# Cross-attention's steps begin behind eight units: the other batches' rows and the null terms move into steps 1 to 7

## The chip, the core and the metric

The kernel runs on one core of a Trainium2 chip. The metric is the time of one execution on the device in microseconds (us), the median of several runs. An engine works through its own queue of instructions in order and waits for semaphores: TensorE (PE in the profile, PEld its weight loads), VectorE (DVE), ScalarE (ACT) and GpSimd (POOL); SyncE (SP) issues most DMAs. PEclk, the granted clock, is the share of TensorE's full clock: 1.00 is 2.4 GHz, 0.50 is 1.2 GHz.

## The reference

One decoder block on `x` (4 batches of 256 rows, width 128) with a context of 512 rows of width 256 for each batch: layer norm, cross-attention with 16 heads of 64 and one learned null key and null value for all heads, a layer norm of its result, a residual sum; then rotary self-attention and a mixture of 8 experts. The change touches cross-attention alone:

```python
kv = jnp.einsum('bmc,cf->bmf', context, Wkv)
k, v = jnp.split(kv, 2, axis=-1)                 # 16 heads of 64
k = jnp.concatenate((nk, k), axis=-2)            # the null key in front
v = jnp.concatenate((nv, v), axis=-2)
sim = jnp.einsum('bhid,bhjd->bhij', q * scale, k)
attn = jax.nn.softmax(sim, axis=-1)
out = jnp.einsum('bhij,bhjd->bhid', attn, v)     # then @ Wout, normalised
```

All products are made in float32 accuracy: each operand is split into a rounded part (`_hi`) and a rest (`_lo`), and three products are added up.

## The kernel before

**The loop.** Cross-attention runs in steps `s` = 0 to 34, one for each pair of heads of a batch (8 pairs, 4 batches), and three to drain. The code writes each engine's queue out by hand; in a step every engine handles pieces of several pairs: scores of pairs s+1 and s+2, transposed probabilities and weighted values of pair s, the query product of pair s+2 (`project_q(s + 2)`), and one *key unit* and one *value unit* of later use (`keys_unit`, `values_unit`: six products of 128x512 each, into one PSUM bank, then a ScalarE copy `_hi` and a rest `_lo`). Its order on TensorE in the second half of a step is: value unit, weighted values of the pair before, whatever a batch needs (`finish_batch`, `null_probs`), transposes, query product, weighted values of this pair (`weighted_values(s, 0)`), scores of pair s+2. Steps that use the out bank for a third purpose put the weighted values ahead of the value unit (`values_late`), and `weighted_values(s, 0)` waits there until that third user is read (`third_user_read`). On VectorE the second half is: o_halves, q_tail(s+2), inverse_sum, `finish_batch`, probs_tail.

**The head.** The *head*, ahead of step 0, is what `class Prologue` holds: loads, the split of the weights into `wkv_hi`/`wkv_lo` in five pieces, layer norm and transposes of the rows, and a list `FIRST` of units that alternate between two banks; a unit waits until VectorE has read the unit two places earlier. `FIRST` holds four key units, four value units and two units "x" that turn the rows of tiles 2 to 7 (batches 1 to 3; batch 0's tiles 0 and 1 go first, `first_tokens`). The head also makes the *null queries* `w0` (null key times Wq), the *null scores* (rows times w0, per tile, kept as `s0n`) and the *null outputs* `u` (null value times Wout), each by products of TensorE. At its end step 0 begins with `keys_unit(0)`.

**Memory.** The raw weights and the head's scratch tiles lie where the loop's `pT_hi`, `o_raw` and others lie later, which is why ScalarE's first o_copy waits for the null outputs and for `wout_lo`.

## Time and profile before

| | us |
|---|---|
| median of 3 runs (lowest, highest) | 642.07 (641.66, 642.63) |
| the profiled execution | 644.23 |
| its span, first to last instruction | 642.4 |
| TensorE busy in the span | 564.4 (88%) |
| VectorE busy | 492.9 (77%) |
| ScalarE busy | 420.5 (65%) |
| GpSimd busy | 327.2 (51%) |

The span is one execution seen by the profiler, with 1.8 us around it. The shares are means over stages with different limits: cross-attention takes about the first 365 us, self-attention and the experts the rest. A row of a timeline gives start, length, engine, line, operation and tiles; the bracket at its end is how long the engine had been idle and who released it.

### The profile page before, as it was taken

The numbers are of one execution on the slowest core, as the hardware profiler recorded it, in microseconds if no ns is written. First come the engines' busy times: TensorE is split into PE (matmuls) and PEld (weight loads), VectorE is DVE, ScalarE is ACT, GpSimd is POOL, SyncE is SP. The second block draws the span as 40 slices with busy tenths as digits, with TensorE's granted clock in tenths as the row PEclk, the third lists the DMA queues.
The fourth block names the chain that finished last, engine by engine and source line by source line (L and its number), as shares of the span: only waits on it lengthen the run. The fifth ranks groups of instructions, "written<-read, shape, count | busy, mean of one in ns | idle before, by whom it ended". The sixth has DMA issues, their size and how long they took to land. (4 is left out here: it accounts for less than half of the span.)

```text
span 642.4 us, 11040 instructions
## 1 busy us (share of the span) xinstructions
PE 564.4 (88%) x3364; PEld 437.0 (68%) x3364; DVE 492.9 (77%) x1037; ACT 420.5 (65%) x1030; POOL 327.2 (51%) x609
## 2 busy tenths in 40 slices
PE   4799889999999898998988558999886699999996
PEld 3467668777777676776866456666555678888885
DVE  4848877887878686978689437898883589999994
ACT  4448767867678766777677427888873355666652
POOL 0517966776677865777766656376963100000000
PEclk9789999999999998999999957999998599999998
DMA  8200010000100000000000020002220000000001
GB/s 297 60 1 2 2 33 2 1 2 2 34 0 2 2 1 0 2 2 2 2 1 2 1 94 1 2 2 87 86 87 2 0 1 1 1 2 1 1 0 34
DMA packets 12186, 13.64 MB, mean 21 GB/s; under 512 B 2144, under 2 KB 10336, under 8 KB 12128
## 3 DMA queue, kind: packets, MB, share of 16 engines
q1 hardware_dynamic: 11664, 12.87, 6.3%
q8 instruction: 28, 0.46, 0.3%
q14 instruction: 30, 0.25, 0.1%
q10 hardware_dynamic: 464, 0.07, 0.1%
HBM read 12.41 MB, written 0.52 MB: 20 GB/s over the span
## 5 line engine op out<-in xcount | busy, mean ns | idle before, releaser
L1166 POOL TENSOR_SCALAR attn_probs<-attn_probs,rinv 128x512 f32<-128x512 f32 x128 | 90.8, 722 | 20.4 <-DVE rinv L1023 20.3
L858 ACT ACTIVATE attn_probs<-bank,bias 128x512 f32<-128x512 f32 x128 | 87.3, 687 | 15.3 <-DVE bias L1016 15.3
L1032 DVE TENSOR_TENSOR pT_lo<-bank,pT_hi 128x512 fp32r<-128x512 f32 x128 | 86.7, 680 | 6.6 <-ACT pT_hi L876 5.0
L688 PE MATMUL bank<-ident,attn_probs 128*128 128x128 f32 x512 | 77.9, 281 | 14.3 <-POOL attn_probs L1166 11.3
L1008 DVE TENSOR_REDUCE neg_max<-bank 128x1 f32<-128x512 f32 x128 | 83.9, 677 | 3.2 <-PE bank L671 3.2
L688 PEld LDWEIGHTS bank<-ident,attn_probs 128*128 128x128 f32 x512 | 55.5, 141 | 41.7 <-POOL attn_probs L1166 25.4
L876 ACT ACTIVATE pT_hi<-bank 128x512 fp32r<-128x512 f32 x128 | 74.2, 595 | 8.8 <-PE bank L688 7.9
L720 PE MATMUL bank<-pT_hi,vals 128*128 128x256 f32 x256 | 65.7, 289 | 2.8 <-DVE pT_lo L1032 2.0
L2008 ACT ACTIVATE act_hi<-act_f 128x512 fp32r<-128x512 f32 x56 | 35.4, 633 | 43.3 <-DVE act_f L2049 43.3
L720 PE MATMUL bank<-pT_lo,vals 128*128 128x256 f32 x256 | 63.6, 282 | 0.0
L720 PEld LDWEIGHTS bank<-pT_hi,vals 128*128 128x128 f32 x256 | 48.4, 189 | 5.4 <-DVE pT_lo L1032 2.6
L1609 ACT ACTIVATE p_raw<-s_pair,neg_max 128x128 f32<-128x128 f32 (+1 forms) x128 | 43.2, 429 | 9.7 <-DVE neg_max L1669 9.5
L720 PEld LDWEIGHTS bank<-pT_lo,vals 128*128 128x128 f32 x256 | 48.4, 189 | 0.8
L1159 POOL TENSOR_TENSOR total<-row_sum,e 128x2 f32<-128x2 f32 x64 | 15.1, 236 | 63.3 <-ACT e L865 60.3
L1042 DVE TENSOR_TENSOR o_sum<-o_raw 64x256 f32<-64x256 f32 x64 | 30.5, 477 | 15.1 <-ACT o_raw L888 13.4
L2053 DVE TENSOR_TENSOR act_lo<-act_f,act_hi 128x512 fp32r<-128x512 f32 x56 | 38.5, 687 | 1.6 <-ACT act_hi L2008 1.0
L2042 DVE TENSOR_TENSOR up_w<-u_bank,wide 128x512 f32<-128x512 f32 x48 | 33.2, 691 | 7.3 <-PE u_bank L1962 1.9
L2049 DVE TENSOR_TENSOR act_f<-up_w,gate 128x512 f32<-128x512 f32 x56 | 38.4, 686 | 0.1
L1186 POOL TENSOR_TENSOR vals<-v_raw,vals 128x512 fp32r<-128x512 f32 x28 | 36.6, 1306 | 2.3
L1669 DVE TENSOR_REDUCE neg_max<-s_pair 128x2 f32<-128x256 f32 x64 | 32.5, 551 | 3.6 <-PE s_pair L1522 3.1
L671 PE MATMUL bank<-keys_hi,q_hi 64*128 64x512 f32 x128 | 32.3, 501 | 3.0 <-ACT attn_probs L858 1.9
L2002 ACT ACTIVATE gate<-g_bank 128x512 f32<-128x512 f32 x56 | 32.6, 582 | 2.4 <-PE u_bank L1962 2.4
(303 smaller groups left out, 1586.8 us busy)
## 6 DMA issues: line engine op xcount, KB each, us to landing
ctx_raw<-in_ctx_T SPq DMA_DIRECT2D x4, 512.0 KB, 3.8
gu_raw<-in_L_ffn_w_gate SPq DMA_DIRECT2D x4, 448.0 KB, 3.5
gu_raw<-in_L_ffn_w_up SPq DMA_DIRECT2D x4, 448.0 KB, 4.4
dn_raw<-in_L_ffn_w_down SPq DMA_DIRECT2D x4, 448.0 KB, 5.3
wkv_raw<-in_L_xattn_Wkv SPq DMA_DIRECT2D x3, 512.0 KB, 9.0
wkv_raw<-in_L_xattn_Wkv SPq DMA_DIRECT2D x2, 256.0 KB, 6.8
wq_raw<-in_L_xattn_Wq SPq DMA_DIRECT2D x1, 512.0 KB, 7.1
wqT_raw<-in_wq_T SPq DMA_DIRECT2D x1, 512.0 KB, 8.2
```

What stands on the lines that cost most here:

```text
L688: last = pe.transpose(t_bank[half][:, j * N + t * P:j * N + (t + 1) * P], probs[:, g % 2, i, t, kt * P:(kt + 1) * P], k.ident[:, :])
L720: last = pe.matmul(o_part, k.vals[:, kt, 2 * (g % HP) + i, :], x[:, i, kt, :], start=kt == 0 and n == 0, stop=kt == KT - 1 and n == 1)
L858: act.activation(probs[:, g % 2, i, t, :], score_bank(G, i)[:, :], ACT.Exp, bias=bias[:, t, h:h + 1], scale=X_SCALE, accum_out=row_sum[:, ...
L876: act.activation(pT_hi[:, i, 2 * half:2 * half + 2, :], t_bank[half][:, :].rearrange("p (j n) -> p j n", j=2), ACT.Copy).then_inc(t_hi_s, 1)
L1008: dve.tensor_reduce(neg_max[:, t, h:h + 1], score_bank(G, i)[:, :], AX_X, ALU.max, negate=True).then_inc(max_s, 1)
L1032: dve.tensor_tensor(pT_lo[:, i, 2 * half:2 * half + 2, :], t_bank[half][:, :].rearrange("p (j n) -> p j n", j=2), f(pT_hi[:, i, 2 * half:2 ...
L1166: pool.tensor_scalar(probs[:, g % 2, i, t, :], probs[:, g % 2, i, t, :], rinv[:, t, h:h + 1], 1.0, ALU.mult, ALU.mult).then_inc(p_norm_s, 1)
L1186: pool.tensor_tensor(values_of(k, i, t, 1), raw, f(values_of(k, i, t, 0)), ALU.subtract).then_inc(v_lo_s, 1)
L1609: last = act.activation(p_raw[:, G % 4, j, t, 0:n], s_bank[(G % 2) * REP + j][:, t * N:t * N + n], ACT.Exp, bias=neg_max[:, t, h:h + 1])
L2008: act.activation(act_hi[:, n % 2, :], act_f[:, n % 2, :], ACT.Copy).then_inc(a_hi_s, 1)
L2049: dve.tensor_tensor(act_f[:, n % 2, :], up_w[:, n % 2, :], gate[:, n % 2, :], ALU.mult).then_inc(mul_s, 1)
L2053: dve.tensor_tensor(act_lo[:, n % 2, :], act_f[:, n % 2, :], f(act_hi[:, n % 2, :]), ALU.subtract).then_inc(a_lo_s, 1)
```

## The change

Five things change; line numbers move with them.

1. `FIRST` is four key units and four value units. The rows of batch 1, 2 and 3 are turned in steps 2, 3 and 4 (`TOKEN_STEPS`): two transposes on TensorE, two copies on ScalarE, a rest on VectorE. The null scores of tiles 2 to 7 are made in step 5, the null outputs in step 7. All use the out bank as a third user, so those steps are `values_late`, and `weighted_values(s, 0)` waits for the VectorE instruction that read it last.
2. The statistics of tiles 2 to 7 end the head on VectorE; GpSimd's inverse deviation for them moves into step 0, the normalisation of the six tiles into VectorE's step 1.
3. In the head, TensorE makes the null queries and the scores of pair 0 before the second key unit; VectorE makes all of `wq_lo` (GpSimd had three quarters); the diagonals of the null key and value are set before `cT_lo`.
4. GpSimd's `output_weights`, `residual_bias` and `self_weights` move from steps 0, 2, 3 to steps 1, 4, 5.
5. The host lays the five pieces of Wkv out so that each partition's part is contiguous, and the null key and value as one array of two columns, loaded by one DMA in place of four. Some scratch tiles move to other memory, and two waits of ScalarE in step 0 go.

```diff
-FIRST = [("k", 0, 0), ("k", 1, 0), ("x", 2, 6), ("k", 2, 0), ("v", 0, 0), ("k", 3, 0),
-         ("v", 0, 1), ("v", 0, 2), ("v", 0, 3), ("x", 6, 8)]
+FIRST = [("k", i, 0) for i in range(KT)] + [("v", 0, t) for t in range(KT)]
...
-        for i in range(2):
-            for which, col in ((0, self.nk_col), (1, self.nv_col)):
-                act.dma_start(col[i * DH:(i + 1) * DH, :], dram["L0_xattn_null_kv"][which, :].rearrange("(d o) -> d o", o=1))\
-                    .then_inc(self.null_in, 16)
+        act.dma_start(self.null_cols[:, :], dram["null_cols"]).then_inc(self.null_in, 16)
...
+        TOKEN_STEPS = {2: 1, 3: 2, 4: 3}
+        NULL_SCORES, NULL_OUTPUTS = 5, 7
+        FIRST_STEPS = (*TOKEN_STEPS, NULL_SCORES, NULL_OUTPUTS)
...
             def third_user_read(s):
 
+                if s in TOKEN_STEPS:
+                    pe.wait_ge(first.xT_lo, TOKEN_STEPS[s] + 1)
+                if s == NULL_SCORES:
+                    pe.wait_ge(first.s0_s, 2)
+                if s == NULL_OUTPUTS:
+                    pe.wait_ge(first.u_lo_s, 1)
...
+            def first_extra(s):
+
+                if s not in FIRST_STEPS:
+                    return
+                pe.wait_ge(o_raw_s, 2 * s)
+                if s in TOKEN_STEPS:
+                    first.turn_tokens(pe, TOKEN_STEPS[s])
+                if s == NULL_SCORES:
+                    first.null_scores(pe, range(QT, TT))
+                if s == NULL_OUTPUTS:
+                    first.null_outputs(pe)
...
-            first.first_tokens(pe)
+            first.turn_tokens(pe, 0)
             first.unit(pe, 0)
             project_q(0)
-            first.unit(pe, 1)
             first.null_queries(pe)
             pe.wait_ge(k.first_lo, 1)
             scores(0, 0)
-            first.null_scores(pe, range(QT), (first.x0_hi, 1)).then_inc(first.null_ps, 1)
+            scores(0, 1)
+            first.null_scores(pe, range(QT))
             project_q(1)
-            scores(0, 1)
-            for n in (2, 3, 4):
+            for n in (1, 2, 3):
                 first.unit(pe, n)
             scores(1, 0)
-            for n in range(5, len(FIRST)):
+            for n in range(KT, len(FIRST)):
                 first.unit(pe, n)
-            pe.wait_ge(first.s0_s, 1)
-            first.null_scores(pe, range(QT, TT), (k.first_hi, len(FIRST)))
-            first.null_outputs(pe)
...
             def finish_batch(s):
+                if s == 1:
+                    first.normal(dve, range(QT, TT), 2)
+                if s in TOKEN_STEPS:
+                    first.tail_tokens(dve, TOKEN_STEPS[s])
+                if s == NULL_SCORES:
+                    first.null_shift(dve, slice(QT, TT), (first.null_ps, 3))
+                if s == NULL_OUTPUTS:
+                    dve.wait_ge(first.u_hi_s, 1)
+                    dve.tensor_tensor(k.u_lo[:, :], first.pU, f(k.u_hi[:, :]), ALU.subtract).then_inc(first.u_lo_s, 1)
...
                 if s == 0:
+                    first.inverse_deviation(pool, slice(QT, TT), 2)
+                if s == 1:
                     output_weights()
-                if s == 2:
+                if s == 4:
                     residual_bias()
-                if s == 3:
+                if s == 5:
                     self_weights()
```

What it moves on the engines is seen at two places. The first is TensorE at the end of the head, from the last value unit (`wkv_hi`, `cT_hi` products) to the first key unit of step 0 (`cT_hi,wkv_hi`). Before:

```order
L86 MATMUL bank<-wkv_hi,cT_hi 128x512
L86 MATMUL bank<-wkv_hi,cT_lo 128x512
L86 MATMUL bank<-wkv_lo,cT_hi 128x512
L230 MATMUL bank<-ident,xn 128x128 x2
L259 MATMUL bank<-w,xnT 128x16 x6
L266 MATMUL bank<-wout_raw,nv_diag 16x128 x8
L84 MATMUL bank<-cT_hi,wkv_hi 128x512
```

And of the change:

```order
L86 MATMUL bank<-wkv_hi,cT_hi 128x512
L86 MATMUL bank<-wkv_hi,cT_lo 128x512
L86 MATMUL bank<-wkv_lo,cT_hi 128x512
L84 MATMUL bank<-cT_hi,wkv_hi 128x512
L84 MATMUL bank<-cT_lo,wkv_hi 128x512
L84 MATMUL bank<-cT_hi,wkv_lo 128x512
```

The last transposes, six matmuls of null scores (each two passes) and eight of null outputs are gone from between them. The second place is VectorE in the second half of steps 1 and 2, from `q_lo` of the query product to `pT_lo` of the probabilities. Before, it reads the same in both steps:

```order
L1042 TENSOR_TENSOR o_sum<-o_raw 64x256 x2
L986 TENSOR_TENSOR q_lo<-bank,q_hi 128x256
L1023 RECIPROCAL rinv<-total 128x2
L1032 TENSOR_TENSOR pT_lo<-bank,pT_hi 128x512
L1008 TENSOR_REDUCE neg_max<-bank 128x1
```

Of the change, step 1 and then step 2:

```order
L994 TENSOR_TENSOR q_lo<-bank,q_hi 128x256
L1031 RECIPROCAL rinv<-total 128x2
L275 TENSOR_SCALAR xn<-x,mean_var,rstd 128x128 x6
L1040 TENSOR_TENSOR pT_lo<-bank,pT_hi 128x512
...
L994 TENSOR_TENSOR q_lo<-bank,q_hi 128x256
L1031 RECIPROCAL rinv<-total 128x2
L235 TENSOR_TENSOR xnT_lo<-bank,xnT_hi 128x256
L1040 TENSOR_TENSOR pT_lo<-bank,pT_hi 128x512
```

The normalisation of six tiles, and in step 2 the rest of the turned rows, stand between the reciprocal and `pT_lo`, behind `q_lo`.

## Rows read from the trace of the kernel before

**Rows 1.** Windows, one per step (steps 1 to 4 and 8); columns in the first line.

```profile
core 0: us, PE busy (x) PEld busy (x) DVE busy (x) ACT busy (x) POOL busy (x), PEclk, DMA share, GB/s
50.50:59.45 8.95, 8.95 (x62) 7.16 (x61) 7.44 (x17) 7.20 (x21) 5.28 (x13) 1.00 0.01 2
59.45:69.12 9.67, 8.81 (x60) 6.99 (x59) 8.71 (x17) 7.28 (x22) 9.21 (x16) 1.00 0.00 1
69.12:79.05 9.93, 9.32 (x63) 7.29 (x61) 8.25 (x17) 7.90 (x22) 9.28 (x19) 1.00 0.01 2
79.05:90.84 11.79, 9.50 (x59) 7.20 (x60) 8.71 (x19) 7.82 (x23) 7.52 (x15) 1.00 0.15 44
...
119.10:128.54 9.44, 9.41 (x63) 7.22 (x62) 7.29 (x17) 7.30 (x22) 6.78 (x16) 1.00 0.00 0
```

**Rows 2.** Timeline of the two transfers' and the context split's start.

```profile
1.17 0.53 ACTq L179 DMA_DIRECT2D nk_col<-in_L_xattn_null_kv  x1
...
6.50 1.23 DVE L1075 TENSOR_TENSOR cT_lo<-ctx_raw,cT_hi 128x1024 fp32r<-128x1024 f32 x1 [0.82 <-ACT cT_hi L918]
```

**Rows 3.** DMA issues: operation, count, KB each, median us from issue to landing.

```profile
nk_col<-in_L_xattn_null_kv ACTq DMA_DIRECT2D x2, 0.2 KB, 5.4
```

**Rows 4.** Timeline of the head and of step 0's first keys.

```profile
12.60 0.39 PE L84 MATMUL bank<-cT_hi,wkv_hi 128*128 128x512 f32 x1
...
13.97 1.85 PE L251 MATMUL bank<-nk_diag,wqT_raw 128*128 128x16 f32 x16
...
17.91 1.84 POOL L1244 TENSOR_TENSOR wq_lo<-wq_raw,wq_hi 128x768 fp32r<-128x768 f32 x1
...
18.23 1.54 DVE L1016 SCALAR_TENSOR_TENSOR bias<-neg_max,s0n 128x2 f32<-128x2 f32 x1
...
44.34 0.69 DVE L993 TENSOR_TENSOR keys_lo<-bank,keys_hi 128x512 fp32r<-128x512 f32 x1 [2.46 <-ACT keys_hi L829]
```

**Rows 5.** VectorE's groups by line and shape, from 0 to 45 us.

```profile
L1008 DVE TENSOR_REDUCE neg_max<-bank 128x1 f32<-128x512 f32 x7 | 4.5, 680 | 0.0
L192 DVE TENSOR_TENSOR wkv_lo<-wkv_raw,wkv_hi 128x1024 fp32r<-128x1024 f32 x3 | 4.1, 1373 | 0.2 <-ACT wkv_hi L186 0.2
L219 DVE TENSOR_TENSOR vals<-bank,vals 128x512 fp32r<-128x512 f32 x4 | 2.7, 686 | 1.4 <-ACT vals L206 1.4
L284 DVE TENSOR_SCALAR xn<-x,mean_var,rstd 128x128 f32<-128x128 f32 x8 | 2.2, 336 | 1.1 <-POOL rstd L298 1.1
L64 DVE BATCH_NORM_STATS2 stats<-x 128x6 f32<-128x128 f32 x8 | 1.7, 282 | 3.2 <-DMA x<-in_x_tiles 3.2
```

**Rows 6.** Timeline of step 8's second half.

```profile
124.86 0.38 PE L756 MATMUL bank<-ident,p 128*16 128x128 f32 x2
...
125.06 0.60 ACT L840 ACTIVATE v_raw<-bank 128x512 f32<-128x512 f32 x1 [0.76 <-PE bank L86]
...
126.17 0.28 PE L720 MATMUL bank<-pT_hi,vals 128*128 128x256 f32 x1
...
126.78 0.42 DVE L986 TENSOR_TENSOR q_lo<-bank,q_hi 128x256 fp32r<-128x256 f32 x1 [1.26 <-ACT q_hi L822]
```

**Rows 7.** Timeline of VectorE and GpSimd in step 15.

```profile
199.10 1.56 DVE L417 TENSOR_SCALAR h_rms<-x,mv_x,to_h 128x128 f32<-128x128 f32 x2
199.19 1.39 POOL L1186 TENSOR_TENSOR vals<-v_raw,vals 128x512 fp32r<-128x512 f32 x1
```

**Rows 8.** Timeline of TensorE in step 14.

```profile
182.94 0.33 PE L688 MATMUL bank<-ident,attn_probs 128*128 128x128 f32 x1 [0.81 <-POOL attn_probs L1166]
```

**Rows 9.** Timeline of TensorE at the head's end.

```profile
37.20 1.48 PE L259 MATMUL bank<-w,xnT 128*128 128x16 f32 x12 [0.84 <-ACT xnT_hi L202]
38.61 2.50 PE L266 MATMUL bank<-wout_raw,nv_diag 128*16 128x128 f32 x16
```

**Rows 10.** Windows with their granted clock, columns as in the first group.

```profile
244.60:248.00 3.40, 1.76 (x12) 1.06 (x13) 3.37 (x8) 2.47 (x6) 2.68 (x4) 1.00 0.00 0
248.02:251.43 3.41, 3.41 (x12) 2.82 (x11) 2.39 (x5) 1.39 (x4) 1.84 (x6) 0.50 0.00 0
```

More of the change, by code:

```diff
@@ L198, in head @@
         act.wait_ge(k.first_ps, n + 1)
-        if kind == "x":
-            cols, got = slice(i * P, t * P), src[:, 0:(t - i) * P]
-            act.activation(self.xnT[:, cols], got, ACT.Copy)
-            last = act.activation(k.xnT_hi[:, cols], got, ACT.Copy)
-        elif kind == "k":
+        if kind == "k":
             last = act.activation(k.keys_hi[:, i, :], src[:, :], ACT.Copy)
@@ L212, in tail @@
         dve.wait_ge(k.first_hi, n + 1)
-        if kind == "x":
-            cols = slice(i * P, t * P)
-            last = dve.tensor_tensor(k.xnT_lo[:, cols], src[:, 0:(t - i) * P], f(k.xnT_hi[:, cols]), ALU.subtract)
-        elif kind == "k":
+        if kind == "k":
             last = dve.tensor_tensor(k.keys_lo[:, i, :], src[:, :], f(k.keys_hi[:, i, :]), ALU.subtract)
@@ L226, in unit, with turn_tokens, copy_tokens, tail_tokens @@
             pe.wait_ge(k.first_lo, n - 1)
-        if kind == "x":
-            pe.wait_ge(self.xn_ready, 2)
-            for tile in range(i, t):
-                last = pe.transpose(out[:, (tile - i) * P:(tile - i + 1) * P], self.xn[:, tile, :], k.ident[:, :])
-        else:
-            piece = VALUES_A if kind == "v" else KEYS_A if i < 2 else KEYS_B
-            pe.wait_ge(self.c0_lo, 1)
-            pe.wait_ge(self.piece_lo, SPLIT_ORDER.index(piece) + 1)
-            last = project(pe, k, kind, i, t, out)
+        piece = VALUES_A if kind == "v" else KEYS_A if i < 2 else KEYS_B
+        pe.wait_ge(self.c0_lo, 1)
+        pe.wait_ge(self.piece_lo, SPLIT_ORDER.index(piece) + 1)
+        last = project(pe, k, kind, i, t, out)
         last.then_inc(k.first_ps, 1)
-    def first_tokens(self, pe):
+    def turn_tokens(self, pe, b):
         pe.wait_ge(self.const_in, 16)
-        pe.wait_ge(self.xn_ready, 1)
+        pe.wait_ge(self.xn_ready, 1 + (b > 0))
         for t in range(QT):
-            last = pe.transpose(self.side[:, t * P:(t + 1) * P], self.xn[:, t, :], self.k.ident[:, :])
-        last.then_inc(self.x0_ps, 1)
+            last = pe.transpose(self.side[:, t * P:(t + 1) * P], self.xn[:, b * QT + t, :], self.k.ident[:, :])
+        last.then_inc(self.xT_ps, 1)
+    def copy_tokens(self, act, b):
+        cols = slice(b * N, (b + 1) * N)
+        act.wait_ge(self.xT_ps, b + 1)
+        act.activation(self.k.xnT_hi[:, cols], self.side[:, 0:N], ACT.Copy)
+        act.activation(self.xnT[:, cols], self.side[:, 0:N], ACT.Copy).then_inc(self.xT_hi, 1)
+    def tail_tokens(self, dve, b):
+        cols = slice(b * N, (b + 1) * N)
+        dve.wait_ge(self.xT_hi, b + 1)
+        dve.tensor_tensor(self.k.xnT_lo[:, cols], self.side[:, 0:N], f(self.k.xnT_hi[:, cols]), ALU.subtract).then_inc(self.xT_lo, 1)
     def null_queries(self, pe):
@@ L252, in null_queries, with null_scores @@
         last.then_inc(self.null_ps, 1)
-    def null_scores(self, pe, tiles, ready):
+    def null_scores(self, pe, tiles):
         pe.wait_ge(self.w0_ready, 1)
-        pe.wait_ge(*ready)
+        pe.wait_ge(self.xT_hi, tiles.stop // QT)
         for t in tiles:
             last = pe.matmul(self.pS0[:, t, :], self.xnT[:, t * P:(t + 1) * P], self.w0[:, :], start=True, stop=True)
-        return last
+        last.then_inc(self.null_ps, 1)
     def null_outputs(self, pe):
@@ L713, in weighted_values @@
                 if g == 0 and i == 0:
[L714 removed]
+                    pe.wait_ge(first.s0_s, 1)
                 m = projected_at(g + 1)
@@ L934, in _ @@
             q_head(1)
-            first.head(act, 2)
+            first.head(act, 1)
             exponential(0, 1, 0)
@@ L1073, in _ @@
             first.normal(dve, range(QT), 1)
+            first.diagonals(dve)
             dve.wait_ge(first.c0_hi, 1)
@@ L1110, in _ @@
             shift(1, 0)
-            for n in range(5, len(FIRST)):
-                first.tail(dve, n)
-                if n == 6:
-                    first.piece_tail(dve, VALUES_B)
-            first.null_shift(dve, slice(QT, TT), (first.u_hi_s, 1))
-            dve.tensor_tensor(k.u_lo[:, :], first.pU, f(k.u_hi[:, :]), ALU.subtract).then_inc(first.u_lo_s, 1)
+            first.tail(dve, KT)
+            first.piece_tail(dve, VALUES_B)
+            first.tail(dve, KT + 1)
+            first.tail(dve, KT + 2)
+            first.tail(dve, KT + 3)
+            dve.wait_ge(first.rest_in, 16)
+            token_stats(dve, range(QT, TT), lambda t: k.x[:, t, :], first.stats, first.mean_var, first.x_var, 4)
             for s in STEPS:
```

129 lines of the change are left out of this document (62 added, 67 removed).

## The prediction

> **What bounds the kernel now.** I read the windows first, one per step of the loop. A regular step takes 8.95 us and TensorE is busy in all of it [rows 1]; steps 5 and 7 look like step 1, and step 6 adds an output projection on both sides of the change. Where a step is longer, TensorE waits: step 2 lost 0.86, step 3 0.61 and step 4 2.29 (length less busy time) [rows 1]. So in these steps work that TensorE gets is paid in full, and so is any wait put in front of it. The head, everything before step 0, is another thing: its timeline shows the engines taking turns, with VectorE's queue as the longest. Its end is read at VectorE's first split of step 0, keys_lo at 44.34 [rows 4]; from there on the two programs do the same until step 1. The chain that ended last reaches back only through the experts at the end and tells nothing of this region.
>
> So the sum has two terms: what the head gives, and what steps 1 to 7 take back.
>
> **The head, up to the first exponential's bias.** The diagonal copies now stand on VectorE ahead of cT_lo, which started at 6.50 when its input came [rows 2], and they wait for one transfer in place of four. It is issued where the first of the four was, at 1.17 [rows 2]; those took 5.4 us to land in the median [rows 3], which gives 6.6, and with the four copies behind it cT_lo starts about 0.8 late. If it lands in half that time the copies are hidden. The Trainium skill, "DMA: Bandwidth & Descriptors", section "Queues, rings and completion order", says that an engine of the DMA takes turns between queues, so that a small transfer need not wait for the large ones of the other queue; by this, and by the fixed 2 us that its section on the anatomy of one DMA gives, the load would be there at about 3.2 and nothing is lost. The trace has 5.4 for such a load and does not bear it out. On the other side the first weight piece comes in longer rows. I take the start as unchanged, with 0 to 1.5 of loss as the bound (a load of 128 rows may take longer than one of 64).
>
> Then the second key unit no longer stands in front of the null queries: they start at 12.60 and not 13.97 [rows 4], and end at 14.45. Two groups of scores follow (about 0.8 each, six products of half height, two side by side, against 1.37 for a unit), and four null scores of 0.12 [rows 9]. VectorE's maxima end by then, since the statistics of the other six tiles (1.3 and some 0.5 for their aggregation [rows 5]) are gone from their front. The bias itself took 1.54 us on 2 elements while GpSimd's wq_lo ran 17.91 to 19.75 [rows 4]; that product is now VectorE's own, in idle time, and the bias should take 0.16. So the bias is ready at about 16.9, not 19.77: 2.9 gained.
>
> **The head, from the bias to keys_lo.** VectorE now has: four maxima (2.7), three weight splits of 1.37 (4.1), three key and four value tails of 0.69 (4.8), six statistics (1.8), one q_lo of 0.42 and five tiny ones (0.8): 14.6 [rows 5, 6]. Consecutive instructions overlap by about 0.07, 1.4 in all. It waits where ScalarE and TensorE are behind: a unit is 1.37 on TensorE and 0.60 on ScalarE [rows 4, 6] and may start only when the tail two units back is done; that leaves 0.5 and 1.0 before the last two values, 0.65 before the last key, 0.6 at q_lo and others, 2.7 in all. So 14.6 - 1.4 + 2.7 = 15.9 us after 16.9: keys_lo at 32.8 to 33, against 44.34. **The head gives 11.3**, all at full clock. Gone from it are the transposes of six tiles, their normalisation, twelve null scores and the null outputs, which ended at 41.1 [rows 9].
>
> **Token steps 2, 3, 4.** Step 8 has the same shape: two transposes of null weights at 124.86, a copy of them, and the step was 0.49 longer than a regular one [rows 1]. There the weighted values started at 126.17, as soon as the query product was out [rows 6]. In a token step they must wait for xnT_lo, and that stands on VectorE behind q_lo and the reciprocal, and q_lo comes out of the query product that TensorE issues after the transposes. In step 8 q_lo ended at 127.20; xnT_lo has its shape (0.42), so it is done at about 127.67, and TensorE stands still for 1.5. ScalarE's two copies fit into its wait for the query product. Behind the waiting weighted values are the next scores and transposes; nothing can pass them. A token step costs 0.5 + 1.5 = 2.0.
>
> **Step 1's normalisation** shows in step 2. Six tiles take 0.28 each [rows 5], but they start beside GpSimd's split of the values. In step 15, at the same place, two such tiles took 1.56, the length of that split [rows 7]. So six take 1.56 + 4 x 0.28 = 2.7, in a step where VectorE has 8.95 - 7.44 = 1.5 idle [rows 1]; 1.2 comes out on TensorE. The nearest wait of that kind is 0.81, in step 14 behind step 13's extra VectorE work [rows 8]. The bounds are 0 (six tiles in the idle time) and 2.7. The Trainium skill, "SBUF — State Buffer", section "Who interferes with whom", has the rule: of VectorE and GpSimd, whichever comes first holds their shared port for its whole instruction. By the head's 0.28 a tile alone this term would be 0.2; by the rule it is the 1.2 of step 15's row, which agrees.
>
> GpSimd's output weights (step 1), bias sum (step 4) and self weights (step 5) move by one or two steps into idle time of GpSimd; step 2 is rid of the bias sum, whose 0.86 is in the old 9.67 [rows 1], and step 4, where TensorE waits anyway, takes it up at nothing.
>
> **The ledger.** Step 2: 8.95 + 2.0 + 1.2 = 12.15 against 9.67, +2.5. Steps 3 and 4: most of step 3's stall falls into the 2.29 that TensorE waits in step 4 anyway; ScalarE's and VectorE's added work pushes that wait by 0.4 (between 0 and 1.5); step 4's own stall is paid, 1.5, while its transposes fit the wait for v_raw: +1.9. Step 5: twelve null scores 1.4 [rows 9], and the weighted values wait for the null shift behind q_lo, 1.03 [rows 6] and some 0.3 for the shift itself after the query product, 1.35: +2.75. Step 7: null outputs of 16 passes 1.8, from 1.85 for the null queries' 16 at full clock [rows 4] (2.50 at half clock [rows 9]), and the same wait for u_lo, 1.35: +3.15. **The steps take 10.3.** So far -1.0.
>
> **The clock.** The trace has granted clock 0.50 from 248.02 to 251.43, right after a stretch in which TensorE was busy 1.76 of 3.40 us [rows 10]; that stretch then did 3.4 us of work at 1.2 GHz in place of 2.4, 1.7 lost. The new program has TensorE standing still for about 1.8 before the third value unit, 1.4 and 1.5 within step 2, and 1.3 to 1.5 in four more places. I count on one such stretch, +1.6, more than before. The sum is then -11.3 + 10.3 + 1.6 = +0.6. The profiled execution, of which all rows are, took 644.23 us: its span of 642.4 and 1.8 around it, 2.2 over the median of the runs, 642.07. I put the difference on the median: **642.7**, and without that stretch 641.1. A difference under 0.2% (1.3 us) can't be told from none here; both lie within it.
>
> **Rivals.** *Faster*: the normalisation doesn't meet GpSimd's split and is hidden (-1.2), and the clock stays: 639.9. For it: the 2.29 of waits in step 4 left the granted clock at 1.00 [rows 1]. Against: step 15's row. A stronger form, that all stalls are hidden and only TensorE's own added work counts (3 x 0.2 + 1.4 + 1.8 = 3.8), gives 642.07 - 11.3 + 3.8 = 634.6; the order of VectorE's queue speaks against it. *Slower, by the clock*: the stretches at 1.2 GHz are two or three. Before the last value units one costs twice 1.2 on VectorE's chain, in step 2 and in step 4 or 5 1.6 each: -1.0 + 2.4 + 1.6 = +3.0, 645.1, and +4.6 with a third. It decides from the second stretch on. For it: the idle times listed. *Slower, by the small load*: it lands late and holds cT_lo and the first unit by 1.5 on top of the forecast: 644.2. For it: 5.4 us for a load of half the rows.
>
> **Chances and range.** No change that can be told 0.39; faster 0.27 (0.24 and 0.03); slower by the clock 0.21, by the load 0.13. So faster 0.27, same 0.39, slower 0.34. The likeliest case by itself reaches from 641 to 643.4. The range takes in the faster rival with some of its bound below, 639.0, and the clock's with a third stretch nearly whole, 646.2; left out are the case without stalls (0.03) and the outer parts of the others, under 0.2 together.
>
> **What would show it.** Right: keys_lo of step 0 near 33; the bias at 0.16 us; token steps in which weighted values wait about 1.5 for xnT_lo; steps 2 to 5 and 7 longer by the ledger; steps from 8 on as before. Wrong: cT_lo waiting for the diagonals; keys_lo past 35, or before 31; weighted values in steps 2 to 7 that wait for nothing; granted clock at 0.50 in more than one stretch between keys_lo and step 8.

## The result, and the profile after

The changed kernel took 649.34 us in the median (647.78 to 649.48), the kernel before 641.87 beside it: a ratio of 1.011, interval 1.009 to 1.0137. A second measurement gave 647.86 against 640.48, ratio 1.010 (1.007 to 1.013). So it is slower by about 7.4 us; 642.7 was forecast, and the range ended at 646.2.

The profiled execution took 647.78 us, span 646.0. That is only 3.6 more than the profiled execution of before, so half of the loss is not in this pair of traces, and the account needs more than one execution of the same program.

**The head.** Timeline of the changed kernel, VectorE, TensorE and the small load; it answers to [rows 2, 4]:

```profile
1.14 0.47 ACTq L170 DMA_DIRECT2D null_cols<-in_null_cols  x1
...
5.67 0.34 DVE L268 COPY nk_diag<-null_cols 64x8 f32<-64x8 f32 x2
6.02 0.35 DVE L268 COPY nv_diag<-null_cols 64x8 f32<-64x8 f32 x2
6.41 1.23 DVE L1092 TENSOR_TENSOR cT_lo<-ctx_raw,cT_hi 128x1024 fp32r<-128x1024 f32 x1
...
8.38 0.76 PE L84 MATMUL bank<-cT_hi,wkv_hi 128*128 128x512 f32 x1 [1.82 <-DVE wkv_lo L182]
8.94 0.63 PE L84 MATMUL bank<-cT_lo,wkv_hi 128*128 128x512 f32 x1
...
11.71 2.11 PE L242 MATMUL bank<-nk_diag,wqT_raw 128*128 128x16 f32 x16
...
16.22 0.16 DVE L1024 SCALAR_TENSOR_TENSOR bias<-neg_max,s0n 128x2 f32<-128x2 f32 x1
...
32.79 0.66 DVE L1001 TENSOR_TENSOR keys_lo<-bank,keys_hi 128x512 fp32r<-128x512 f32 x1
```

And its DMA issues (operation, count, KB, median us from issue to landing), answering to [rows 3]:

```profile
null_cols<-in_null_cols ACTq DMA_DIRECT2D x1, 1.0 KB, 4.2
```

keys_lo of step 0 starts at 32.79, where before had 44.34. The diagonals are done before `cT_lo` can start. The 0.63 of the second product is a reading lesson of its own: the same product takes 0.39 to 0.40 later on. TensorE begins at half clock, and here the null queries, 2.11 where 1.85 is full clock, show the change-over in their midst. The kernel before begins the same way; [rows 4] start only behind it:

```profile
9.90 0.63 PE L84 MATMUL bank<-cT_lo,wkv_hi 128*128 128x512 f32 x1
```

**The steps.** Windows of the changed kernel; each runs from the end of one query product to the end of the next, columns as in [rows 1]. The 32 query products are counted from 0; product 2 ends at 36.48, product 10 at 128.05. Product g is issued in step g-2, and the stall behind it falls into the next window. [rows 1] have other bounds.

```profile
36.48:45.39 8.91, 8.91 (x60) 7.11 (x60) 7.76 (x15) 7.18 (x19) 7.77 (x12) 1.00 0.00 1
45.39:56.59 11.20, 9.77 (x62) 7.17 (x60) 10.57 (x24) 7.97 (x21) 6.96 (x14) 1.00 0.00 0
56.59:67.64 11.05, 9.60 (x62) 7.38 (x61) 7.58 (x17) 7.93 (x21) 6.66 (x14) 1.00 0.01 2
67.64:81.10 13.46, 11.55 (x61) 8.47 (x61) 10.14 (x19) 9.14 (x23) 10.03 (x15) 0.87 0.14 40
81.10:92.94 11.84, 10.42 (x72) 8.49 (x71) 8.08 (x17) 7.38 (x19) 9.51 (x21) 1.00 0.00 1
92.94:106.22 13.28, 12.03 (x74) 9.92 (x74) 7.32 (x17) 7.77 (x20) 5.70 (x12) 0.87 0.01 2
106.22:117.13 10.91, 10.91 (x75) 8.26 (x74) 7.40 (x17) 7.34 (x20) 7.03 (x17) 1.00 0.01 2
117.13:128.05 10.92, 9.62 (x63) 7.53 (x64) 7.40 (x17) 7.54 (x20) 6.45 (x14) 1.00 0.00 0
```

The two windows with a granted clock of 0.87 each hold a half-clock stretch. A later trace of the same kernel (648.76 us, below) has none in these steps, so that its lengths show the work and the waits alone. Two of its windows (products 5 to 6 and 7 to 8), and two of the kernel before in the same bounds (3 to 4 and 6 to 7):

```profile
72.39:85.24 12.85, 10.13 (x61) 7.54 (x61) 10.12 (x19) 9.11 (x23) 10.01 (x15) 1.00 0.14 42
97.07:108.92 11.85, 10.60 (x74) 8.86 (x74) 7.32 (x17) 7.76 (x20) 5.69 (x12) 1.00 0.01 2
```

```profile
57.22:66.14 8.92, 8.92 (x61) 7.12 (x61) 7.70 (x16) 7.18 (x19) 8.46 (x15) 1.00 0.01 2
88.62:97.55 8.93, 8.93 (x62) 7.13 (x61) 7.33 (x16) 7.18 (x19) 6.38 (x13) 1.00 0.00 1
```

| from query product | before | change, 1st trace | change, trace of 648.76 | last less before |
|---|---|---|---|---|
| 2 to 3 | 8.93 | 8.91 | 8.92 | 0.0 |
| 3 to 4: normalisation, first rows turned | 8.92 | 11.20 | 11.16 | +2.2 |
| 4 to 5: step 2's stall, bias sum gone | 9.81 | 11.05 | 11.05 | +1.2 |
| 5 to 6: step 3's stall, the old wait | 12.67 | 13.46 | 12.85 | +0.2 |
| 6 to 7: step 4's stall, null scores | 8.93 | 11.84 | 11.83 | +2.9 |
| 7 to 8: step 5's stall | 10.38 | 13.28 | 11.85 | +1.5 |
| 8 to 9: null outputs | 8.93 | 10.91 | 10.90 | +2.0 |
| 9 to 10: step 7's stall | 9.47 | 10.92 | 10.91 | +1.4 |
| sum | 78.04 | 91.57 | 89.47 | +11.4 |

Behind product 10 the trace of 648.76 is as before to 0.3 us up to product 21.

**The stalls.** Timeline of the changed kernel where the windows grew: the normalisation, a token step (2), the null scores' step (5) and the null outputs' (7), answering to [rows 5 to 9]:

```profile
42.06 2.44 POOL L1235 TENSOR_TENSOR wout_lo<-wout_raw,wout_hi 128x1024 fp32r<-128x1024 f32 x1
...
43.42 1.10 DVE L1024 SCALAR_TENSOR_TENSOR bias<-neg_max,s0n 128x2 f32<-128x2 f32 x1
...
46.50 2.99 DVE L275 TENSOR_SCALAR xn<-x,mean_var,rstd 128x128 f32<-128x128 f32 x6
46.62 1.35 POOL L1199 TENSOR_TENSOR vals<-v_raw,vals 128x512 fp32r<-128x512 f32 x1
...
51.60 1.32 PE L686 MATMUL bank<-ident,attn_probs 128*128 128x128 f32 x8 [1.18 <-POOL attn_probs L1179]
...
57.04 0.42 DVE L994 TENSOR_TENSOR q_lo<-bank,q_hi 128x256 fp32r<-128x256 f32 x1 [0.92 <-ACT q_hi L835]
...
57.46 0.40 DVE L235 TENSOR_TENSOR xnT_lo<-bank,xnT_hi 128x256 fp32r<-128x256 f32 x1
...
58.01 0.36 PE L724 MATMUL bank<-pT_hi,vals 128*128 128x256 f32 x1 [1.42 <-DVE xnT_lo L235]
...
94.19 0.55 PE L724 MATMUL bank<-pT_hi,vals 128*128 128x256 f32 x1 [1.25 <-DVE s0n L282]
...
114.27 1.92 PE L257 MATMUL bank<-wout_raw,nv_diag 128*16 128x128 f32 x16
...
118.40 0.36 PE L724 MATMUL bank<-pT_hi,vals 128*128 128x256 f32 x1 [1.27 <-DVE u_lo L1061]
```

The bracket of the weighted values names the last reader of the out bank, which stands on VectorE behind q_lo; steps 3 and 4 show the same 1.42. The first two rows are of step 1: GpSimd's output weights, which item 4 of the change moved there, run beside VectorE's bias, and it takes 1.10 where the bias takes 0.14 to 0.19 in the steps around.

**The clock.** Windows of the changed kernel around three half-clock stretches, each with what TensorE did just before, answering to [rows 10]:

```profile
67.00:70.25 3.25, 1.82 (x13) 1.51 (x13) 1.67 (x5) 3.11 (x10) 2.42 (x5) 1.00 0.00 0
70.27:73.68 3.41, 3.41 (x14) 2.22 (x16) 2.33 (x6) 2.03 (x6) 2.14 (x4) 0.50 0.00 0
90.75:94.15 3.40, 2.19 (x20) 1.98 (x18) 1.79 (x6) 1.86 (x6) 2.68 (x6) 1.00 0.00 0
94.16:97.57 3.41, 3.38 (x14) 2.61 (x14) 0.50 (x1) 1.50 (x5) 0.72 (x2) 0.50 0.02 7
217.05:220.45 3.40, 1.47 (x10) 1.02 (x9) 1.90 (x4) 0.64 (x2) 2.38 (x4) 1.00 0.00 0
220.46:223.87 3.41, 3.41 (x17) 3.23 (x16) 1.06 (x3) 2.31 (x9) 2.08 (x4) 0.50 0.00 0
```

The first follows step 3's stall of 1.42 and the second step 5's of 1.25; the third follows a wait of 1.93 at 219.75 for self-attention's operand `hT_lo`, which is 1.64 in the kernel before. By the table the first two cost 0.6 (13.46 less 12.85) and 1.4 (13.28 less 11.85). Such a wait does not bring a stretch by itself: in the trace of 648.76 the same three, of 1.42, 1.25 and 1.89, pass at full clock.

### The profile page after: what moved, and what is told of

Read it like the earlier page. It is cut to its first block and busy times, and to the rows that moved or that the text cites. A ratio compares the mean times of both kernels' runs of the same rounds, so it can differ in the third digit from the quotient of the medians.

```text
span 646.0 us, 11044 instructions
## 1 busy us (share of the span) xinstructions
PE 565.8 (88%) x3364; PEld 438.4 (68%) x3364; DVE 492.9 (76%) x1039; ACT 420.9 (65%) x1032; POOL 325.0 (50%) x608
## 5 line engine op out<-in xcount | busy, mean ns | idle before, releaser
L1016 DVE TENSOR_REDUCE neg_max<-bank 128x1 f32<-128x512 f32 x128 | 83.8, 676 | 11.8 <-PE bank L669 11.6
L686 PE MATMUL bank<-ident,attn_probs 128*128 128x128 f32 x512 | 79.2, 284 | 14.3 <-POOL attn_probs L1179 11.8
L724 PE MATMUL bank<-pT_hi,vals 128*128 128x256 f32 x256 | 67.7, 296 | 9.5 <-DVE xnT_lo L235 4.2
L724 PE MATMUL bank<-pT_lo,vals 128*128 128x256 f32 x256 | 65.0, 286 | 0.0
L994 DVE TENSOR_TENSOR q_lo<-bank,q_hi 128x256 fp32r<-128x256 f32 x32 | 13.6, 424 | 31.8 <-ACT q_hi L835 31.7
```

Source lines behind the costliest of these rows:

```text
L686: last = pe.transpose(t_bank[half][:, j * N + t * P:j * N + (t + 1) * P], probs[:, g % 2, i, t, kt * P:(kt + 1) * P], k.ident[:, :])
L724: last = pe.matmul(o_part, k.vals[:, kt, 2 * (g % HP) + i, :], x[:, i, kt, :], start=kt == 0 and n == 0, stop=kt == KT - 1 and n == 1)
L1016: dve.tensor_reduce(neg_max[:, t, h:h + 1], score_bank(G, i)[:, :], AX_X, ALU.max, negate=True).then_inc(max_s, 1)
```

## The experiments

**More traces of the same programs.** The changed kernel was run again unaltered, once for time and trace and three times for a trace alone; the kernel before once, for time and trace.

> The changed kernel unaltered, once more, for a second trace beside those below. My account so far: head -11.8 us, steps 2 to 8 +10.6 of work and waits, and the rest half-clock stretches of TensorE, +1.3 to 1.7 each. By it the time is about 649 again, steps 2 to 8 hold two or three such stretches, and the position at the end of step 8's query product is 128 to 130 us. Rival: the surplus over the first trace's +3.6 lies in the later stages (self-attention, experts); then that position is 128.0 as before and the span is longer only behind 365 us.

> The kernel before unaltered, for a second trace. Its first trace took 644.2 us, 2.2 over the median of its runs, and held half-clock stretches from 22.7 to 29.6, 39.8 to 43.2 and 248.0 to 251.4 us ahead of the experts. If the surplus of the timed difference (+7.4) over that of the two traces (+3.6) is only that the first trace of before was an unlucky one, the second trace is shorter, about 640 us, and lacks one or more of these stretches. Rival: it has the same stretches and 644 us again; then the surplus is in the kernel of the change.

> The changed kernel unaltered, for its trace alone. Theory: a time of 644 to 648 us goes with a head whose products run at full clock from about 12 us (query product of step 0 out at 36.5 us), a time of 648.5 to 652 with one that has full clock only from about 24.5 (out at 40.7 to 41.1). Rival: a slower execution has the head as in the first traces and more half-clock stretches in the steps or behind them.

> As for the run before it: the changed kernel unaltered; full clock in the head from about 12 us with a time of 644 to 648, or from about 24.5 with one of 648.5 to 652.

> As for the two runs before it: the changed kernel unaltered; full clock in the head from about 12 us with a time of 644 to 648, or from about 24.5 with one of 648.5 to 652.

The change: 647.86 (644.82 to 649.24, 6 executions), its trace 647.73 with product 10 at 128.1 and half clock at 70.1 and 83.8: two stretches in steps 2 to 8, as the account said, and the median and the trace are within 0.2 of each other. The kernel before: 642.21 (641.19 to 644.63, 8), its trace 644.63 with the same stretches as the first one. So the surplus was not an unlucky trace of before; that expectation fell.

The three single traces took 648.76, 645.41 and 645.62. The slowest of them has the other head, as forecast: the *late head*, in which full clock comes at 24 us, against the *early head* with full clock from 12 us. Its timeline of TensorE:

```profile
8.92 0.76 PE L84 MATMUL bank<-cT_hi,wkv_hi 128*128 128x512 f32 x1 [1.83 <-DVE wkv_lo L182]
...
12.26 3.43 PE L242 MATMUL bank<-nk_diag,wqT_raw 128*128 128x16 f32 x16
...
20.13 0.63 PE L84 MATMUL bank<-cT_hi,wkv_hi 128*128 128x512 f32 x1
...
23.97 0.46 PE L84 MATMUL bank<-cT_hi,wkv_hi 128*128 128x512 f32 x1
24.27 0.39 PE L84 MATMUL bank<-cT_lo,wkv_hi 128*128 128x512 f32 x1
```

All of the head's first products run at half clock until 24.1 us (0.63 for a product, 3.43 for the null queries). Query product 2 ends at 41.26, against 36.45 to 37.03 in the four other traces of this kernel: 4.2 to 4.8 us. It has no other half-clock stretch up to 362 us; the traces of 645.4 and 645.6 have two and three, from 70 to 221 us, and so it ends only 3.1 to 3.4 behind them.

**The moved work left out**, twice (the edit leaves out the turning and normalising of the rows of batches 1 to 3, their null scores, and the null outputs; every batch uses batch 0's rows, and a constant stands for `u`):

```diff
-        TOKEN_STEPS = {2: 1, 3: 2, 4: 3}
-        NULL_SCORES, NULL_OUTPUTS = 5, 7
+        TOKEN_STEPS, NULL_SCORES, NULL_OUTPUTS, FIRST_STEPS = {}, None, None, ()
```

> All work that the change moves out of the head is left out of the steps too: no rows of batches 1 to 3 are turned or normalised (every batch uses batch 0's rows), null scores of batch 0 alone, no null outputs (a constant in their place); statistics and GpSimd's three moved pieces stay. This gives what the shorter head is worth by itself. By my account the head gives 11.8 and the bias sum gone from step 2 another 0.9, so 629 to 630 us and steps 1 to 8 like those of before. Rival: part of it is given back later whatever the steps do (half-clock stretches that come with the earlier start): 632 to 635.

> The kernel with the moved work left out, once more (no rows of batches 1 to 3 turned or normalised, null scores of batch 0 alone, no null outputs), for a second trace of a kernel whose executions lay between 629 and 640 us. If the scatter is TensorE's clock, a slower execution shows either the head's first products at half clock beyond 12 us (4.5 us longer, as one trace of this head showed), or more half-clock stretches in the steps; the span less these is 627 again. Rival: waits differ between executions (transfers that land late), at the same clock.

The traces took 629.26 and 635.75. In the first, product 2 ends at 36.84, and from product 6 to product 21 it is 12.4 to 12.6 us ahead of before: the head's 11.5 and 1.2 in steps 2 to 4, where 0.9 was expected. In the second, product 2 ends at 41.03; its null queries say why:

```profile
11.73 3.43 PE L242 MATMUL bank<-nk_diag,wqT_raw 128*128 128x16 f32 x16
```

Of the 6.5 us between them 4.2 are this head; a half-clock stretch at 239.3 makes another 1.6. The timed executions of both runs lay at 629.0 to 639.8; the first run's median is 634.5 (633.5 without its two slowest), ratio 0.9925 (0.9894 to 0.9957). So the median lies in the rival's 632 to 635: part of the head's gain goes to the clock although no moved work is there to stall on.

**The reads ahead of q_lo.** VectorE's order alone; the null shift and u_lo move with the rest of the rows:

```diff
                 o_halves(s - 1, 1)
+                if s in TOKEN_STEPS:
+                    first.tail_tokens(dve, TOKEN_STEPS[s])
...
                 q_tail(s + 2)
```

> The third user's read on VectorE (xnT_lo in steps 2 to 4, the null shift in step 5, u_lo in step 7) stands ahead of q_lo instead of behind it and the reciprocal. By the ledger TensorE's stall ahead of the weighted values shrinks from 1.42 to about 0.35 in the three token steps and from 1.25 to 0 in steps 5 and 7: -5.7 us against the change, and if the half-clock stretches of steps 3 and 5 follow those stalls another -1.5 to -3.2, so 640 to 643.5. Rival one, the wait only passes to the next thing (q_lo comes later, scores wait): -2 or less, 647 or more. Rival two, the stretches at half clock come whatever the stalls: -5.7 and no more, 643.5.

642.62 (638.31 to 646.50, 11 executions), ratio to before 1.0033 (1.0004 to 1.0063); the change beside it 647.86, so -5.2. Timeline of step 2:

```profile
56.58 0.42 DVE L235 TENSOR_TENSOR xnT_lo<-bank,xnT_hi 128x256 fp32r<-128x256 f32 x1 [0.38 <-ACT xnT L229]
...
57.12 0.42 DVE L994 TENSOR_TENSOR q_lo<-bank,q_hi 128x256 fp32r<-128x256 f32 x1
...
57.15 0.36 PE L724 MATMUL bank<-pT_hi,vals 128*128 128x256 f32 x1 [0.48 <-DVE xnT_lo L235]
```

The stall is 0.48 in place of 1.42 (0.35 was expected) and gone in steps 5 and 7; nothing took its place. This trace (638.53) has no half-clock stretch ahead of 213.9 us, and product 10 ends 7.1 us ahead of the change's first trace (120.94 against 128.05). Between products 2 and 10 it takes 84.35, where the trace of 648.76 takes 89.47: so 5.1 were waits, of the 5.7 expected, and 2.1 were the first trace's two stretches. That the stretches go with these waits is not shown: the median's -5.2 is near rival two's -5.7, and other kernels keep full clock with the waits in place (below).

**The normalisation dealt out**, two tiles each ahead of q_lo in steps 1 to 3:

```diff
-                if s == 1:
-                    first.normal(dve, range(QT, TT), 2)
...
+                if 1 <= s < B:
+                    first.normal(dve, tiles_of(s), 2)
                 q_tail(s + 2)
```

> The normalisation of six tiles is dealt out, two tiles each in steps 1, 2 and 3, and stands ahead of q_lo, where VectorE is idle for about 0.9 us and GpSimd has not begun its split of the values. By the shared-port reading the wait of 1.18 us of TensorE in step 2 (transposes waiting for the normalised probabilities) is gone and nothing comes in its place: -1.2 us against the change, about 648. Rival: what costs is VectorE's amount of work in these steps and not GpSimd's split; then the two tiles ahead of q_lo delay it by up to 0.56 in each of the three steps and the time stays at 649 or is longer.

649.63 (645.39 to 651.92, 6): no gain; its trace has the late head. But the rival's reason is not it either. VectorE and GpSimd in its steps 1 and 2:

```profile
50.67 1.88 DVE L275 TENSOR_SCALAR xn<-x,mean_var,rstd 128x128 f32<-128x128 f32 x2
60.65 0.60 DVE L275 TENSOR_SCALAR xn<-x,mean_var,rstd 128x128 f32<-128x128 f32 x2
```

```profile
50.33 0.78 POOL L1197 TENSOR_SCALAR vals<-v_raw 128x512 fp32r<-128x512 f32 x1
51.20 1.26 POOL L1199 TENSOR_TENSOR vals<-v_raw,vals 128x512 fp32r<-128x512 f32 x1
```

In step 1 VectorE comes so late that even this place lies beside GpSimd's two instructions on the values: the two tiles take 1.88 (0.52 and 1.43, each ending 0.1 behind one of GpSimd's), q_lo waits behind them, and TensorE stood still for 1.96. VectorE is late because its bias at 48.04 took 1.06 beside GpSimd's output weights (46.65 to 49.08), as in the change. In step 2 the same two tiles take 0.60 and cost nothing: products 4 to 5 take 11.07, in the change 11.05. What is priced is the meeting, not the tiles. The Trainium skill, "SBUF — State Buffer", section "Who interferes with whom", says that when VectorE runs in a mode that uses two ports, of it and GpSimd the one that comes first keeps the shared port for its whole instruction; these rows agree.

**The null outputs back in the head:**

```diff
+            pe.wait_ge(first.s0_s, 1)
+            first.null_outputs(pe)
             for s in STEPS:
```

> The null outputs go back to the head's end, as before the change; all else as in the change. By the ledger step 7 loses 1.8 of TensorE's work and 1.25 of waiting, -3.0, and the head's end gets the 16 passes, of which TensorE, which waits there for VectorE's tails, pays 0 to 1.9, and step 0's weighted values wait for the rest of it in the out bank: -1.1 to -3.0 against the change, 645 to 647. Rival: they cost as much in the head (TensorE's end of the head is the bound there too): 648 again.

646.36 (640.62 to 649.20, 12), ratio 1.0054 (1.0027 to 1.008), 1.5 to 3 below the change. In its trace products 8 to 9 and 9 to 10 take 8.93 and 9.47 again, 3.4 less, and product 2 ends at 42.33, 1.2 later than the other traces with half clock until 24 us (41.03 to 41.26). So the term was sound on both sides: 3.4 in step 7, 1.2 in the head.

**All stalls attacked.** ScalarE first copies the turned rows out of the bank and TensorE waits for that copy alone; two tiles are normalised ahead of q_lo in steps 2, 3 and 4, and so the rows are turned in steps 3 to 5 and the null scores made in step 6; the null shift and u_lo stand ahead of q_lo. Of the edit, the steps and TensorE's wait:

```diff
-        TOKEN_STEPS = {2: 1, 3: 2, 4: 3}
-        NULL_SCORES, NULL_OUTPUTS = 5, 7
+        TOKEN_STEPS = {3: 1, 4: 2, 5: 3}
+        NULL_SCORES, NULL_OUTPUTS = 6, 7
...
-                    pe.wait_ge(first.xT_lo, TOKEN_STEPS[s] + 1)
+                    pe.wait_ge(first.xT_raw, TOKEN_STEPS[s])
```

> All stalls attacked: in token steps ScalarE copies the turned rows out of the bank first and TensorE waits for that copy alone (hi and lo are made from the copy), two tiles each are normalised ahead of q_lo in steps 2, 3 and 4 (not in step 1, where GpSimd's split is already under way), rows are turned in steps 3 to 5, null scores are made in step 6, and the null shift and u_lo are read ahead of q_lo. By the ledger steps 2 to 8 then cost only TensorE's own added work, 3 x 0.25 + 1.4 + 1.8 = 4.0, and the old wait of step 4: -6.6 against the trace of the change without half-clock stretches, so a trace of 634 to 636 and a median 1 to 2% below the change, 638 to 641, at or under the kernel before. Rival: stalls that the clock takes anyway; then a median of 643 to 645.

640.48 (637.59 to 646.54, 12), ratio 1.0009 (0.998 to 1.0039): as fast as before, in two groups: seven executions at 637.6 to 640.5, five at 643.8 to 646.5. Its trace (638.45, where 634 to 636 was expected) has the early head and one stretch in the steps, at 70.1; products 2 to 10 take 85.3, 4.2 less than 89.47 where 6.6 less was expected. The rival's 643 to 645 is the upper group and not the median, which is at the upper end of the forecast.

**TensorE kept busy in the head.** Products of a tile of zeros, 128x128, into a bank that is not in use, 15 ahead of the rows' transposes and 6 ahead of the first key unit (the trace counts two matmuls for each), in the change and in three other kernels (in one of them the moved work is left out, as above):

```diff
+            first.keep_busy(pe, 15)
             first.turn_tokens(pe, 0)
+            first.keep_busy(pe, 6)
             first.unit(pe, 0)
```

> TensorE is kept busy in the head from about 1.2 us with 21 products of a tile of zeros (128x128) into a bank that is free, 15 ahead of the rows' transposes and 6 ahead of the first key unit; all else as in the change. Theory: in some executions the new head's first products run at half clock until 24.5 us and not 12.1 (three traces of eight; 4.2 us), and this is what spreads the times of the change. Then full clock is there before the first unit in every execution, the head is 1 to 2 us shorter than in the fast case, and the median falls from 648 to 644 to 646. Rival: the scatter comes from later stretches; then the median is 647 to 648.

> The same products of zeros in the kernel with all stalls attacked, whose executions lay at 637.6 to 640.5 and at 643.8 to 646.5. Theory: the upper group is the head at half clock until 24.5 us; it goes, and the rest gains 1 to 2: median 636.5 to 638.5, below the kernel before by 0.5%. Rival: both groups stay, median 640.

> The same products of zeros in the kernel with the moved work left out (no rows of batches 1 to 3 turned or normalised, null scores of batch 0 alone, no null outputs), whose executions lay between 629 and 640. Theory: 627 to 629 with less scatter, and the head's worth in every execution is the 12 to 13 us of the trace. Rival: median 632 or more.

> The same products of zeros in the kernel before. Both its traces have full clock at 12.5 us, and half clock from 22.7 to 29.6 and 39.8 to 43.2 us. Theory: its head is bound by VectorE's queue and its clock comes in time in every execution, so early products at full clock give 0 to 1 us, 640 to 642. Rival: the early clock is worth as much there as in the change, 1.5 to 2 us or more.

| | without | with | ratio to before |
|---|---|---|---|
| the change | 647.86 | 641.00 (639.17 to 644.89, 12) | 0.998 (0.997 to 1.000) |
| all stalls attacked | 640.48 | 635.22 (632.77 to 639.89, 6) | 0.989 (0.987 to 0.991) |
| moved work left out | 634.47 | 630.71 (627.95 to 630.85, 4) | 0.983 (0.981 to 0.984) |
| before | 641.99 | 640.04 (639.45 to 642.42, 8) | 0.997 (0.996 to 0.999) |

TensorE's timeline in the change with them:

```profile
0.97 5.94 PE L242 MATMUL bank<-idle_tile 128*128 128x128 f32 x30 [0.97 <-POOL idle_tile L1259]
...
8.36 0.47 PE L84 MATMUL bank<-cT_hi,wkv_hi 128*128 128x512 f32 x1
8.67 0.40 PE L84 MATMUL bank<-cT_lo,wkv_hi 128*128 128x512 f32 x1
```

The medians without are those of the runs above; that of before is the one beside these runs. The first key unit runs at full clock, and product 2 ends at 34.64, 1.8 ahead of the early head and 6.6 ahead of the late one. The change gains 6.9 in the median, more than the 2 to 4 expected, and its executions now lie within 6 us below 645. Before gains 1.9, the rival's size, so 5 of the 6.9 are the change's own. The kernel with all stalls attacked gains 5.3 and is 1.1% under before; with the moved work left out the scatter shrinks from 10 us to 3, at 2 us over the forecast.

The head is not all that changes. In this trace of the change the stalls are as before (products 2 to 10 take 89.53, against 89.47 at full clock), but the stretches near 70, 84 or 94 and 220 us are gone; one at 159.5 is the only one between 5.9 and 357 us. And the products do not keep the clock up everywhere: the trace of the kernel with all stalls attacked and the products (639.89, the slowest of its six) has half clock from 13.6 to 20.5 us, and product 2 ends at 38.08.

The Trainium skill, "TensorE: Matmul & The Clock Gate", section "What's actually happening", puts it as "the default state is throttled, and activity releases the throttle"; the first key unit's 0.40 here in place of 0.63 agrees.

**What in the head decides.** First, the first key unit waits for the first part of `wq_lo`, to start as late as before; second, the 6 products ahead of that unit without the 15:

```diff
             first.turn_tokens(pe, 0)
+            pe.wait_ge(first.wq_lo_s, 1)
             first.unit(pe, 0)
```

```diff
             first.turn_tokens(pe, 0)
+            first.keep_busy(pe, 6)
             first.unit(pe, 0)
```

> TensorE waits for the first part of wq_lo ahead of the first key unit, which then starts at about 9.3 us, where before has it; all else as in the change. Theory A, it is the earlier start that meets the clock badly in some executions: those go, the head ends 0.5 to 0.9 later than in the fast case, all executions at 644.5 to 646.5, median 645.5. Theory B, the start has nothing to do with it: both kinds stay, up to 650, median 647 to 649.

> Only the 6 products of zeros between the rows' transposes and the first key unit, without the 15 ahead of them. If the idle time of 1.8 us in that place decides, full clock comes by 12 us in every execution and the median is 643.5 to 645.5, no execution above 647. If the early products are what counts, the slow kind stays: median 647 to 649.

The later start: 645.01 (640.74 to 648.80, 7). Two of seven, 647.2 and 648.8, lie above theory A's band and one below it, so it is not shown; the unit also started at 8.93 in the trace and not at 9.3. The six products alone: 641.79 (640.90 to 646.06, 12), ten of them under 643.2, with 643.5 to 645.5 forecast. Filling the 1.8 us of idle time ahead of the first unit gives nearly all that the 21 products give, 6.1 of 6.9. In its trace full clock comes at 10.5, product 2 ends at 35.83, products 2 to 10 take 89.50, and again the one stretch ahead of 358 us is at 160.7.

One execution of the later start, its traced one, tells more than the median does. Its windows from full clock to query product 2 and from there to product 10:

```profile
37.12:126.57 89.45, 79.88 (x523) 62.25 (x522) 66.15 (x141) 62.10 (x163) 59.88 (x115) 1.00 0.02 7
13.10:37.12 24.02, 21.56 (x115) 15.70 (x115) 19.39 (x45) 14.29 (x31) 6.76 (x16) 1.00 0.20 62
```

Full clock from 13.05 to 357.8 us, without a stretch; steps of 89.45, as in the trace of 648.76; 640.74 us in all.

## Why the prediction was wrong

**The head, -11.3: right, where the clock comes early.** Product 2 ends 11.3 to 11.8 us ahead of before in four traces of the change. keys_lo at 32.79 lies on the forecast 32.8 to 33, and the bias took 0.16. That keys_lo meets the forecast so closely is in part luck: the bias was ready at 16.38, 0.5 ahead of its forecast, and the stretch from it to keys_lo took 16.4 where 15.9 was summed. The small load landed in 4.2 us, not 5.4, and held nothing up: that rival is out. The clause "all at full clock" is taken up below.

**The steps, +10.3: right in place, short by 1.1.** The stalls of 1.42 (forecast 1.5) in the token steps and of 1.25 and 1.27 (1.35) in steps 5 and 7 came where the order of VectorE's queue had put them, and the reordering took them away. By the table steps 2 to 4 took 2.2 + 1.2 + 0.2 and step 4's 1.42, 5.1 (4.4 forecast); step 5 took 2.9 + 1.5 less that 1.42, 3.0 (2.75); step 7 took 3.4 (3.15). Step 3's stall did vanish into step 4's old wait: +0.2. The mis-sized term is the normalisation: the window it falls in is 2.2 longer, of which 0.25 to 0.5 are the transposes, so it cost TensorE some 1.7 to 2.0 and not 1.2. Two things stand behind it. Six tiles held VectorE for 2.99, not 2.7. And the output weights, which the prediction let move into step 1 as GpSimd's idle time, held VectorE's bias for 0.9 more just ahead of them: the meeting that the prediction saw in the head, with `wq_lo`, and overlooked here. By themselves they cost TensorE nothing (with the moved work left out the bias takes 0.92 there and the same window 8.98); how much they add to the normalisation was not tested. A slip without effect: the 2.50 of [rows 9] for the null outputs is only partly at half clock, which began at 39.80; at full clock they took 1.92 in step 7, with 1.8 summed.

**The clock, +1.6: the step that failed.** "I count on one such stretch" and, for the head, "all at full clock". What the clock took:

- In the head, 4.2 to 4.8 us in those executions in which TensorE stays at half clock until 24 us. One of five traces of the change shows it, and three of six of other kernels with the same start. The first rows of [rows 4] began at 12.60, behind the change-over; the products just ahead of them, at 0.63, show that the head has a clock to earn.
- In steps 2 to 8, none to two stretches of 0.6 to 1.5 each, after the new stalls (two in three of the five traces). The rival "slower, by the clock" named such places, at 1.6 each; at its third place, before the last value units, the clock falls in none of the five, and it knew nothing of the head's beginning or of what lies behind step 8. The sign of being wrong that the prediction had set itself, more than one stretch between keys_lo and step 8, is there in those three.
- At 220.5 us, some 1.6 (products 18 to 20 took 24.62 where before took 23.06), in four of the five traces; before does not have this stretch.

Trace against trace the change is 3.6 longer, where 0.6 was forecast: the head gave 0.5 more, the steps took 1.1 more, and the clock took 2.1 in the steps and 1.6 at 220.5 where 1.6 was summed, which leaves 0.3. Median against median it is 7.4. The products of zeros show that TensorE's clock is most of that: they take the change from 1% over the kernel before to level with it (1.0 over, 641.00 against 640.04, where both have them), and 5 of the 6.9 us that they give back are the change's own. How this divides between the late head and the stretches behind it is not shown, since both are gone in the traces of the change with these products; which executions without a trace had the late head is not known either.

The sum without a stretch, 641.1, is near the 640.74 of the one execution at full clock up to 357.8 us, but not for the reasons given: head and steps there (-11.2 and +11.4) leave it 0.2 behind the trace of before at product 10. It comes out ahead because before loses 1.3 more between products 10 and 31, where its own stretch at 248 lies, and because what stands behind product 31, the last, took 2.5 less.

**What stays open.** Why the same program gets full clock at 12 us in one execution and at 24 in another, and why the same wait is followed by half clock in one and not in another. Both traces of before (644.23 and 644.63) lie 2.2 and 2.4 over its medians, so a pair of traces understates the loss by that much; why is not shown. And the part behind product 31, whose work no kernel here changes, took 296.1 to 301.5 us in the traces (298.5 in both of before): a scatter as large as most differences told of here.

## What to carry to other kernels

Where a stage gets shorter at a program's start, look at what its first products take beside the same product later: a shorter head can be paid back in TensorE's clock, and filling idle time ahead of the first product was worth 6.1 to 6.9 us here. A bank that is handed from one user to the next is free when its last reader is through its own queue: put that read ahead of what does not block anybody, or have one engine copy the bank out first. Before moving work into an engine's idle time, ask which other engine it meets there. Judge by several traces and by the spread of the runs, since one pair of traces hid half of this loss. With the stalls attacked and the products of zeros the change's idea beats the kernel before by 1.1%, 635.22 against 641.99 (by 0.8% against the kernel before with the same products, 640.04).

## What was not expected of the hardware

- The profile's record of the clock begins only when the first full clock is granted. In the trace of 648.76 the window from 12.46 to 24.10 shows PEclk 1.00 while a 128x512 product takes 0.63. The durations tell, not the column:

```profile
12.46:24.10 11.64, 11.64 (x45) 9.69 (x45) 5.76 (x13) 4.31 (x12) 0.55 (x3) 1.00 0.48 151
```

- One program, two heads: full clock from 12.1 to 13.1 us or from 24.1 to 24.7, and nothing between, in fourteen traces of heads without products of zeros.
- Two tiles of 128x128 on VectorE take 0.60 by themselves and 1.88 beside GpSimd's two instructions on the values.
- An instruction of VectorE on two elements a partition, the bias, takes 0.14 to 0.19 in most steps, 1.10 beside GpSimd's output weights and 1.54 beside its `wq_lo` [rows 4].
